# Graph attention and expert layers on one core: in the softmax stage, the sum of x and the output bias moves from VectorE to GpSimd, and the carry-on key moves ahead of the wait for the dot products

## The reference

```python
Q, K, V = (n @ W for W in (Wq, Wk, Wv))                   # n = layernorm(x), 8 heads of 32
score = (Q[src] * K[tgt]).sum(-1) * scale + edge_attr @ We  # one score per edge and head
m = segment_max(score, tgt)
ex = exp(score - m[tgt])
attn = ex / segment_sum(ex, tgt)[tgt]
agg = segment_sum(attn[..., None] * V[tgt], tgt)
x = x + agg.reshape(N, 256) @ Wo + bo                     # x + bo is what this change touches
```

## Time and profile before

| what | value |
|---|---|
| time, median of 3 runs | 2590.65 us (2589.32 to 2593.04) |
| the profiled execution's own time | 2574.81 us |
| its span (first to last instruction) | 2573.1 us |
| the softmax stage in it | about 748 to 822 us |
| granted clock of TensorE, mean | 0.758 of full speed |

### The profile page before, as it was taken

How to read it: one execution, slowest core, us unless ns; L and a number is a source line. 1 busy time by engine, 2 the same in 40 slices (tenths; PEclk the granted TensorE clock), 3 DMA queues, 4 the chain that set the end, 5 groups by cost and what they waited for, 6 DMA issues and landing times. The chain is left out here.

```text
span 2573.1 us, 36837 instructions
## 1 busy us (share of the span) xinstructions
PE 1501.0 (58%) x8905; PEld 1231.4 (48%) x8906; DVE 1129.5 (44%) x2738; ACT 759.5 (30%) x1808; POOL 1103.9 (43%) x1149
## 2 busy tenths in 40 slices
PE   6617888888842889599920000000027739999992
PEld 3305666666632555499910000000016639999991
DVE  6516777777757511311153333333345851212113
ACT  2315556555520333234410000000001213343440
POOL 4156777777721200122206777777760002222220
PEclk9857778878865999799965555555558659999996
DMA  6167555555552000366645666666640129999997
GB/s 176 48 144 178 154 154 157 154 154 154 153 123 62 21 20 10 107 202 197 196 115 180 208 211 207 207 205 206 210 152 8 50 93 343 336 346 342 327 343 188
DMA packets 265946, 439.97 MB, mean 171 GB/s; under 512 B 36936, under 2 KB 204504, under 8 KB 265783
## 3 DMA queue, kind: packets, MB, share of 16 engines
q1 hardware_dynamic: 203427, 289.63, 35.1%
q0 software_dynamic: 56368, 146.82, 19.6%
q10 hardware_dynamic: 6116, 3.13, 0.7%
HBM read 347.85 MB, written 91.58 MB: 171 GB/s over the span
## 5 line engine op out<-in xcount | busy, mean ns | idle before, releaser
L1687 POOL DMA_INDIRECT fr<-f_rows,src_s x420 | 404.5, 963 | 183.5 <-issue 117.1
L698 POOL DMA_INDIRECT qr<-q_rows,src_s x420 | 405.7, 966 | 159.8 <-issue 121.1
L1970 PE MATMUL psO<-acc,carry_on 128*125 128x256 f32 x50 | 23.1, 647 | 612.8 <-DVEq L1866 600.1
L1707 DVE SCALAR_TENSOR_TENSOR acc<-acc,same,fr 128x256 f32<-128x256 f32 x420 | 203.9, 485 | 335.7 <-DMA fr<-f_rows,src_s 286.9
L1970 PEld LDWEIGHTS psO<-acc,carry_on 128*125 128x125 f32 x50 | 15.7, 327 | 619.8 <-DVEq L1866 600.5
L793 PE MATMUL psK<-kp,oh_k 126*128 x1680 | 306.8, 349 | 0.0
L793 PEld LDWEIGHTS psK<-kp,oh_k 126*128 126x128 bf16 x1680 | 204.8, 122 | 93.3 <-issue 10.2
L1508 PEld LDWEIGHTS m1psH<-m1xT,m1w 128*128 128x128 f32 x1792 | 211.2, 194 | 2.8
L1508 PE MATMUL m1psH<-m1xT,m1w 128*128 128x128 f32 x1792 | 211.4, 277 | 0.0
L1520 PE MATMUL m1psY<-m1w,m1hT 128*128 128x256 f32 x896 | 203.9, 381 | 2.1 <-DMA m1b<-in_L_ffn_b_dram 1.8
L1488 ACT ACTIVATE m1hT<-m1psH,m1par 128x128 f32<-128x128 f32 x448 | 128.0, 368 | 251.5 <-PE m1psH L1508 251.5
(11 more groups left out here) (429 smaller groups left out, 2389.1 us busy)
## 6 DMA issues: line engine op xcount, KB each, us to landing
m1w<-in_L_ffn_W_dram SPq DMA_DIRECT2D x112, 1024.0 KB, 7.6
run_rows<-acc SPq DMA_DIRECT2D x84, 640.0 KB, 3.5
m0w<-in_L_ffn_Wd_dram SPq DMA_DIRECT2D x32, 1024.0 KB, 5.5
loc<-locals_ SPq DMA_DIRECT2D x85, 157.5 KB
ea<-in_edge_attr_dram SPq DMA_DIRECT2D x84, 140.0 KB
yt<-y SPq DMA_DIRECT2D x15, 560.0 KB
m1b<-in_L_ffn_b_dram SPq DMA_DIRECT2D x56, 128.0 KB, 8.9
qr<-q_rows,src_s POOLq DMA_INDIRECT x420
```

The source lines that it names most:

```text
L698: nc.gpsimd.indirect_dma_start(out=qr[:, g, u, :], out_offset=None, in_=q_rows, in_offset=bass.IndirectOffsetOnAxis(ap=src_s[:, g, u:u + 1 ...
L1687: nc.gpsimd.indirect_dma_start(out=fr[:, g, u, :], out_offset=None, in_=f_rows, in_offset=bass.IndirectOffsetOnAxis(ap=src_s[:, g, u:u + 1 ...
L1707: ins = nc.vector.scalar_tensor_tensor(acc[:, g, u, :], acc[:, n // G % GI, n % G, :], same[:, bass.ds(i * GI * G + g * G + u, 1)], fr[:, ...
```

## The change

VectorE no longer adds `bo` to `x_sb`. GpSimd does it with one instruction of the same size, behind its ramp, once x and the bias have landed; it raises a new semaphore `s_xbo`, and VectorE waits for that at the place where it made the sum. The key block moves up from behind line 1013 to ahead of the wait for `dot`. So that its data are there, the fill of `next_i` moves ahead of the fill of `dot`, and SyncE loads `next_i` before `dot`. SyncE's own wait for `dot` to land, which stood ahead of the loads of x and the bias, is gone.

```diff
             def _(sp):
-                sp.wait_ge(s_dotz, 1)
-                for a, b in ((0, 112), (112, ET)):
-                    sp.dma_start(dot[a:b], dot_rows.rearrange("h (p j) -> p h j", p=ET)[a:b]).then_inc(s_dot, 16)
                 sp.wait_ge(s_next, 1)
...
-                sp.wait_ge(s_dot, 32)
+                sp.wait_ge(s_dotz, 1)
+                for a, b in ((0, 112), (112, ET)):
+                    sp.dma_start(dot[a:b], dot_rows.rearrange("h (p j) -> p h j", p=ET)[a:b]).then_inc(s_dot, 16)
                 for a, b in HALVES:
                     sp.dma_start(x_sb[a:b], rows_of_tiles(x)[a:b]).then_inc(s_xback, 16)
                 sp.dma_start(bo[:], L0_gnn_bo.partition_broadcast(P)).then_inc(s_xback, 16)
             def _(pool):
                 nc.gpsimd.iota(carry_on[:], pattern=[[P, T], [1, P]], base=0, channel_multiplier=0,
                                allow_small_or_imprecise_dtypes=True).then_inc(s_targets, 1)
+                pool.wait_ge(s_xback, 48)
+                nc.gpsimd.tensor_tensor(x_sb[:], x_sb[:], bo[:].unsqueeze(1).to_broadcast([P, T, D]), ALU.add).then_inc(s_xbo, 1)
             def _(v):
+                nc.vector.memset(next_i[:], -1).then_inc(s_next, 1)
                 nc.vector.memset(dot[96:E], 0.0).then_inc(s_dotz, 1)
-                nc.vector.memset(next_i[:], -1).then_inc(s_next, 1)
...
                 link(nc.vector.tensor_scalar(first[:], first[:], -1.0, BIG, ALU.add, ALU.mult))
+                v.wait_ge(s_next, 33)
+                link(nc.vector.tensor_copy(next_f[:], next_i[:]))
+                link(nc.vector.tensor_tensor(key[:, 0:1], dst_f[:, J - 1:J], next_f[:], ALU.is_equal))
+                link(nc.vector.tensor_scalar(key[:, 1:2], dst_f[:, J - 1:J], 1.0, None, ALU.add))
+                link(nc.vector.tensor_tensor(key[:, 1:2], key[:, 1:2], key[:, 0:1], ALU.mult))
+                link(nc.vector.tensor_scalar(key[:, 1:2], key[:, 1:2], -1.0, None, ALU.add))
+                v.wait_ge(s_targets, 1)
+                nc.vector.tensor_scalar(carry_on[:], carry_on[:], key[:, 1:2], None, ALU.is_equal).then_inc(s_cont, 1)
                 v.wait_ge(s_dot, 32)
...
-                v.wait_ge(s_next, 33)
-                link(nc.vector.tensor_copy(next_f[:], next_i[:]))
-                link(nc.vector.tensor_tensor(key[:, 0:1], dst_f[:, J - 1:J], next_f[:], ALU.is_equal))
-                link(nc.vector.tensor_scalar(key[:, 1:2], dst_f[:, J - 1:J], 1.0, None, ALU.add))
-                link(nc.vector.tensor_tensor(key[:, 1:2], key[:, 1:2], key[:, 0:1], ALU.mult))
-                link(nc.vector.tensor_scalar(key[:, 1:2], key[:, 1:2], -1.0, None, ALU.add))
-                v.wait_ge(s_targets, 1)
-                nc.vector.tensor_scalar(carry_on[:], carry_on[:], key[:, 1:2], None, ALU.is_equal).then_inc(s_cont, 1)
...
-                v.wait_ge(s_xback, 48)
-                link(nc.vector.tensor_tensor(x_sb[:], x_sb[:], bo[:].unsqueeze(1).to_broadcast([P, T, D]), ALU.add))
+                v.wait_ge(s_xbo, 1)
                 v.wait_ge(s_over, 1)
```

More of the change, by code:

```diff
@@ L887, in build @@
         s_rowsT, s_lr, s_lrT = (sem(n) for n in ("rows_turned", "reach_made", "reach_turned"))
-        s_dotz = sem("dots_zeroed")
+        s_dotz, s_xbo = sem("dots_zeroed"), sem("x_and_bias")
         s_dot, s_xback, s_targets, s_m, s_ex, s_sums, s_sumst, s_over = (sem(n) for n in (
```

## The result

The changed kernel is slower, by 0.4%. In 20 runs each, side by side, its median is 2594.51 us (2590.67 to 2604.57) against 2586.4 us of the kernel before (2577.87 to 2595.5). The ratio is 1.0038, 95% interval 1.0026 to 1.0050: about 9.8 us, between 6.7 and 12.9 (the two medians lie 8.1 us apart; the ratio is not taken from them). The prediction stood on the first three runs of before, whose median was 2590.65; with all twenty it is 4.3 us lower, so of the 8.2 us between the predicted 2602.7 and the measured 2594.51, 4.3 are the base and not the change.

The account below looks back on a forecast made before the run. No engine is busy for even 60%, so the stage's own longest chain, mostly VectorE, counts. Terms -2.7 + 0 + 0.5 + 14.3 = +12.1 us; from a 2590.65 us median, 2602.7 us, range 2587.5 to 2610.

Parts of the forecast that it names:

- The key block, -2.7: Moved from just before the running sums into VectorE's 5.95 us wait for `dot`, it costs 0 there: -2.7 us.
- The sum taken off VectorE, 0: The sum of x and bias ran beside TensorE's 10.67 us of matmuls, so removing its 6.80 us gains 0.
- The earlier load of x, +0.5: Issued right behind `dot` in SyncE's queue, x delays only `dot`'s last packets: +0.5 us; x and bias land between 775 and 777.
- The sum on GpSimd, +14.3: GpSimd's sum, begun in the reverse maxima, makes VectorE's next two-SBUF-input instruction wait its full length: +14.3 us, bounds 0 and 19.2.
- the first case: GpSimd's sum holds the shared SBUF path for the whole instruction: +12.1 us in total, median 2602.7 us; chance 0.56.
- the rival of a part-time hold (+6.8): GpSimd's sum holds the path only for its reads, 9.0 us, or piecewise: +6.8 us, 2597.4 us; chance 0.14.
- side by side: GpSimd's reads pass between VectorE's and no VectorE instruction is held: 2588 to 2588.5 us; chance 0.20.
- x beside `dot`: The early load of x delays `dot` by up to 7 us, no instruction held: up to +4.3, 2595 us; chance 0.04.
- The rival that GpSimd is kept out: GpSimd gets the path only after the running sums, about 808, so the stage's end waits for it: 2592.0 us; chance 0.06.
- The signs given in advance: Timeline marks: key block over by 761, GpSimd's sum starting 775 to 777, a 14 us scan or idle stretch, `over` copied near 833.

Follow-up runs that it names:

- the versions with one input: Against the changed kernel, bias sum back on VectorE behind GpSimd, which adds 0.0 to x (stage 85.24 us) or copies x onto itself (75.51 us).
- beside the PSUM copy: Changed kernel, but GpSimd's sum also waits until TensorE has turned four columns, so it begins beside a VectorE fill and PSUM copy; stage 82.46 us.

## Why the prediction was right

**The key block, -2.7: right.** It measured -2.71 in the changed kernel and -2.66 alone. The loads of `next_i` were there in time: the block began at 761.46, right behind the preparation, and ended 3.3 us ahead of `dot`. My bound for their landing was never needed.

**The sum taken off VectorE, 0: right.** The copy of `over` still begins 0.1 us behind TensorE's last matmul; the freed time stands in the row as 10.83 us of idle time, where I had worked out 10.91.

**The earlier load of x, +0.5: too high.** It measured +0.29 in the one execution, of which 0.12 is the later fill of `dot` (its loads begin 3.75 us behind the ramp, 3.63 before), and nothing over all versions. That x and the bias would be there between 775 and 777 was right: 781.85 less the 5.03 us by which this stage began later is 776.8.

**The sum on GpSimd, +14.3: the mechanism right, the size 0.9 us too large.** The held scan cost 13.41 us. The length of the instruction was estimated from fills and selects as 14.3; alone it is 13.7. The recorded 14.17 begins while a scan is still running, so it probably contains a short wait of GpSimd's own. That 14.3 came so near was partly luck: it adds 0.84 ns for the write and 0.70 for each read, and this rule fails for the versions with one input. The copy, a read and a write, takes 0.86 ns an element, no more than a fill (11.77 us for 4 x 3360, 0.88 each), and the addition of a constant takes 2.56. The step from one direction (rows 7: GpSimd waits for VectorE) to the other, which no row of before showed, held: the versions with the sum alone and beside the PSUM copy show it directly.

**The sum of terms.** +12.1 forecast, +11.0 in the stage, 9.8 (6.7 to 12.9) in the runs. The runs alone don't decide between the first case and the rival of a part-time hold (+6.8), which their interval just contains; that rival is refuted by the 14.42 us scan, side by side by the same row, and x beside `dot` by the version with the key block alone. The rival that GpSimd is kept out didn't occur: it was let in between two scans that follow each other without any wait. The signs given in advance have to be read from the stage's start, which lay 5.03 us later in that execution: the copy of `over`, announced near 833, stood at 837.20, that is at 832.2.

No version beats the kernel before by a margin that its runs can show. The best, the key block alone, has the shorter stage by 2.7 us.

## What to carry to other kernels

Work that is already hidden behind another engine gains nothing by moving, and on GpSimd it can cost its whole length: before moving a sum there, look at which instructions of VectorE will run beside it, and with what operands. If VectorE's own chain is the path and has two SBUF inputs per instruction, nearly the whole duration of a long GpSimd instruction that reads SBUF is added to the path, in whichever VectorE instruction comes next; cut into 25 pieces the same work still cost 9.2 us of 13.4. A hole in front of a wait, as the 5.95 us ahead of `dot`, is where small work from the path belongs; the gain is as small as the work, here 2.7 us of the stage, too little to be seen in the kernel's time.

## What the runs showed of the hardware

- GpSimd's durations don't follow from the count of inputs: over 125 x 6400 f32 elements a copy took 5.52 us (0.86 ns an element), an addition of two tensors 13.7 (2.14), and an addition of a constant to one tensor 16.4 (2.56), the slowest of the three.
- A fill on GpSimd, which reads nothing, held a VectorE copy of 8 elements for 1.5 us and a `tensor_scalar` of 384 elements for 2.8 us, and left scans and two-input sums untouched.
- SyncE's issue of the two loads of x took 12.28 us when it followed the loads of `dot` directly, against 5.65 us before, and 5.50 with the wait kept. What stood behind it on SyncE waited, here the load of the bias, issued at 770.37; GpSimd's sum, and not VectorE's chain, waited for that load.
